# Moving one elementwise operation of the last layer's scans from GpSimd to VectorE

## What is computed

```python
xs  = jnp.stack([xf, xf[..., ::-1], xt, xt[..., ::-1]], axis=1)      # (b, 4, 192, 3136)
dbc = jnp.einsum('bkcl,krc->bkrl', xs, x_proj_w)
dlt, b, c = (dbc[:, :, :R], dbc[:, :, R:R + N], dbc[:, :, R + N:])   # R = 6, N = 16
dlt = jnp.einsum('bkrl,kdr->bkdl', dlt, dt_proj_w) + dt_proj_b[None, :, :, None]
dlt = jax.nn.softplus(dlt)
dA  = dlt[..., None] * A_log[None, :, :, None, :]
phi = jnp.exp(-jnp.cumsum(dA, axis=3))
dbx = dlt[..., None] * jnp.swapaxes(b, 2, 3)[:, :, None] * xs[..., None]
h   = phi * jnp.cumsum(dbx / (phi + 1e-12), axis=3)
y   = jnp.einsum('bkdln,bknl->bkdl', h, c) + Ds[None, :, :, None]
```

## Time and profile before

| | us |
|---|---|
| median of 3 runs | 17136.74 |
| lowest and highest | 17131.63, 17143.35 |
| the profiled execution, its own time | 17136.74 |
| its span, first to last instruction | 17135.0 |
| layer 3's scans, steady stretch of the first pair | 11320 to 13865 |
| layer 3's scans, steady stretch of the second pair | 14292 to 16846 |
| DVE, POOL, PE, ACT busy, share of the span | 89%, 77%, 80%, 70% |

### The profile page before, as it was taken

How to read it: one execution, slowest core, us unless ns; L and a number is a source line. 1 busy time by engine, 2 the same in 40 slices (tenths; PEclk the granted TensorE clock), 3 DMA queues, 4 the chain that set the end, 5 groups by cost and what they waited for, 6 DMA issues and landing times. The chain is left out here.

```text
span 17135.0 us, 184002 instructions
## 1 busy us (share of the span) xinstructions
PE 13644.1 (80%) x38048; PEld 5622.1 (33%) x38048; DVE 15278.8 (89%) x20463; ACT 12036.7 (70%) x24501; POOL 13160.7 (77%) x6369
## 2 busy tenths in 40 slices
PE   7989978888888878888888886977777776777776
PEld 2222233333333333333333333533332332333323
DVE  6666579999999988999999996889999988999998
ACT  3555666667777756666777774578888867888886
POOL 0000069999999978999999994279999977999996
PEclk9999989999999989999999997988888888888898
DMA  1000023333333333333333332222222212222221
GB/s 24 18 14 16 5 87 107 108 107 107 107 107 107 106 93 103 107 108 106 108 107 106 107 107 76 58 73 85 83 81 82 82 48 78 84 83 82 81 82 46
DMA packets 543166, 1404.61 MB, mean 82 GB/s; under 512 B 135566, under 2 KB 191926, under 8 KB 539430
## 3 DMA queue, kind: packets, MB, share of 16 engines
q1 hardware_dynamic: 542034, 1392.84, 28.1%
HBM read 1311.24 MB, written 58.30 MB: 80 GB/s over the span
## 5 line engine op out<-in xcount | busy, mean ns | idle before, releaser
L1067 PE MATMUL PS<-Hc,ident 128*128 128x448 f32 x16128 | 7355.8, 589 | 1945.7 <-POOL Hc L1381 1690.4
L1373 POOL TENSOR_TENSOR Tr<-du,BC 128x1344 f32<-128x1344 f32 x2688 | 8164.8, 3038 | 34.5 <-DVE du L1252 34.4
L1067 PEld LDWEIGHTS PS<-Hc,ident 128*128 128x128 f32 x16128 | 3079.1, 202 | 6125.1 <-POOL Hc L1381 2668.8
L1189 ACT ACTIVATE PS<-dl,A 128x448 f32<-128x448 f32 x5376 | 3402.8, 633 | 2047.8 <-DVE Hr L1290 1247.9
L1381 POOL TENSOR_TENSOR Hc<-Hr,BC 128x448 f32<-128x448 f32 (+1 forms) x2688 | 3895.5, 1449 | 627.2 <-DVE Hr L1290 548.0
L1290 DVE TENSOR_TENSOR_SCAN PS<-PS,st,Tr 128x448 f32<-128x448 f32 x3072 | 3358.5, 1135 | 132.3 <-ACT st L1203 130.1
L1297 DVE TENSOR_TENSOR Hc<-PS,BC 128x448 f32<-128x448 f32 x4480 | 2564.8, 605 | 0.0
L1197 ACT ACTIVATE PS<-cs,lneps,A 128x448 f32<-128x448 f32 x2688 | 1940.1, 722 | 199.3 <-DVE PS L1290 196.1
L1273 DVE SCALAR_TENSOR_TENSOR PS<-PS,Tr 128x448 f32<-128x448 f32 x2688 | 1646.4, 613 | 224.7 <-ACT PS L1197 214.2
L1189 ACT ACTIVATE Ar<-dl,A 128x448 f32<-128x448 f32 x2688 | 1765.0, 657 | 0.0
L1290 DVE TENSOR_TENSOR_SCAN Hr<-PS,st,Tr 128x448 f32<-128x448 f32 x1536 | 1750.4, 1140 | 0.0
(11 more groups left out here) (268 smaller groups left out, 16212.9 us busy)
## 6 DMA issues: line engine op xcount, KB each, us to landing
BC<-bcscratch SPq DMA_DIRECT2D x5376, 224.0 KB, 3.6
zscratch<-zst SPq DMA_DIRECT2D x84, 224.0 KB, 1.9
bcscratch<-rows SPq DMA_DIRECT2D x336, 56.0 KB, 2.9
z<-zscratch SPq DMA_DIRECT2D x28, 672.0 KB, 4.9
xg<-mid SPq DMA_DIRECT2D x12, 1176.0 KB, 7.9
xr<-mid SPq DMA_DIRECT2D x56, 168.0 KB, 2.8
rl<-rows SPq DMA_DIRECT2D x56, 168.0 KB, 3.3
Q<-part SPq DMA_DIRECT2D x72, 98.0 KB, 4.3
```

Source lines behind the costliest of these rows:

```text
L1067: e.matmul(PS[:, YB + c, 0:T], K["ident"][:], Hc[:, g % NHC, c, :], start=False, stop=(nn == 15)).then_inc(y_done, 1)
L1189: e.activation(decay_at(u), dl[:, q % 2, c, :], ACT.Exp, scale=A[:, q // NT, c, nn:nn + 1]).then_inc(a_done, 1)
L1373: e.tensor_tensor(Tr[:, g % NTR], du[:, q % 2], b, ALU.mult).then_inc(t_done, 1)
```

## The change

`one_less` moves from POOL's program (r = 7) to DVE's (s = 22, which is r = 7, c = 1: behind `scan(g, 1)` and before `project(g, 0)`). The instruction, its operands and its semaphores are the same. `prepare` of DVE is called for tile 0 too, for s = 0 to 47.

```diff
@@ dve @@
+            def one_less(q):
+
+                e.wait_ge(expd, 3 * (q + 1))
+                if q:
+                    e.wait_ge(x_full, use(q - 1, "total", 2) + 1)
+                e.tensor_scalar(w1[:], du[:, q % 2], 1.0, 1.0, ALU.add, ALU.subtract).then_inc(minus, 1)
+
...
             def prepare(q, s):
-                if s in (32, 36, 41):
+                if ratio and s == 22:
+                    one_less(q)
+                elif s in (32, 36, 41):
                     (cumsum if ratio else inputs)(q, (32, 36, 41).index(s))
@@ pool @@
-            def one_less(q):
-
-                e.wait_ge(expd, 3 * (q + 1))
-                if q:
-                    e.wait_ge(x_full, use(q - 1, "total", 2) + 1)
-                e.tensor_scalar(w1[:], du[:, q % 2], 1.0, 1.0, ALU.add, ALU.subtract).then_inc(minus, 1)
-
             def prepare(q, r):
-                if ratio and r == 7:
-                    one_less(q)
                 if ratio and 11 <= r < 14:
                     inputs(q, r - 11)
```

## The result

| | us |
|---|---|
| changed kernel, median of 4 runs | 17279.85 |
| the kernel before, median of 4 runs beside it | 17134.19 |
| ratio | 1.0084, 95% interval 1.0069 to 1.0098 |
| so slower by | 144 (118 to 168) |
| spans of the two profiled executions | 17272.7 and 17135.0, difference 137.7 |

The account below looks back on a forecast made before the run. The prediction took DVE to set the pace. 54 held instructions at 2.75 us (+148.5) less 7.7 us in the beginnings gave +141 us on 17136.7, so 17277.5 us, 0.8% slower; range 17200 to 17330.

Parts of the forecast that it names:

- DVE sets the pace, POOL's saving is worth nothing: In the steps, 54 x 4.74 us = 256 us of POOL's time removed, all beside DVE's, so nothing on the path.
- The instruction itself: On DVE, the 128x1344 `tensor_scalar` takes 0.89 us, costing 0.81 us if nothing holds it.
- The rival of the slow rate: On DVE, the instruction runs at the slow rate and isn't held: 1.48 us each, +72 us, 17209; chance 0.08.
- The hold: On DVE, the instruction waits 2.09 us for POOL's `input1`, so the next starts 2.75 us later.
- The delay goes through whole: Behind it in the steps, ACT's block moves too and the 2.96 us pause stays: 54 x 2.75 = +148.5 us.
- The beginnings: At each pair's start, for tile 0, it ends 3.86 us sooner on idle DVE; two times, -7.7 us.
- The rival of the pause: The delay hides in DVE's 2.96 us pause a step later, so steps cost nothing: 17129 us; chance 0.06.

Follow-up runs that it names:

- the thin `one_less`: Against the kernel before: `one_less` stays on POOL but computes 3 of the 1344 columns, the others set to zero once per pair; 17133.95 us, ratio 0.9993.
- the padded `w1`: Changed kernel with two unused columns behind each group of 448 in `w1`; 17207.95 us, ratio 1.0042 against the kernel before.
- s = 21: Changed kernel with `one_less` on DVE one group earlier, behind scan(g, 0); 17202.65 us, ratio 1.0033 against the kernel before.
- s = 23: Changed kernel with `one_less` on DVE one group later, behind scan(g, 2); 17135.67 us, ratio 0.9992 against the kernel before.
- s = 25: Changed kernel with `one_less` on DVE in step r = 8, behind scan(g, 1), before DVE's pause; 17135.51 us, ratio 0.9994 against the kernel before.

## Why the prediction was right

**DVE sets the pace, POOL's saving is worth nothing.** Right as far as can be told: the run with the thin `one_less` gains 12 us (27 to a loss of 3), some 8 of them in the beginnings, and in the changed kernel POOL's idle time grew and the time with it. The share of busy time had POOL ahead; the waits were the view that decided.

**The instruction itself.** 0.89 us from the line between two lengths; measured 0.86 unheld in the beginnings, 0.83 behind a scan. The rival of the slow rate was refused in part because the profile shows the three groups as 1344; this was no argument, since the padded `w1` is printed as 1344 as well.

**The hold.** Expected to end 0.74 us after `input1`, it ends 0.71 after it; 2.75 us of path became 2.73. Both rows it was read from, a 192-element instruction beside a memset and a short one of the convolution stage, carried over to another shape and stage. The Trainium skill's page "SBUF — State Buffer", section "Who interferes with whom", states the exclusion of such a DVE instruction and a GpSimd instruction, first come first served. The positions s = 21, 22 and 23 agree in who waits for whom: DVE 0.6 and 2.0 us, then POOL 0.5. In one point the measurement differs: held, the instruction ends 0.71 us after POOL's, less than its own 0.86, so what is exclusive isn't the whole of the length that the profile shows.

**The delay goes through whole.** Right in the place: the pause is 2.97 us as before, and the block of ACT starts behind the same scan. The steps of the first pair are 75 us longer and those of the second 71, where 74 each were forecast. The small waits are 6 us shorter in the changed kernel's trace, a term that the sum didn't have; its cause is open, as said above.

**The beginnings.** 3.86 us each were expected, 3.66 measured. PE does begin 3.95 us sooner after the table load (1.02 us behind it instead of 4.97), but from there to DVE's first `input2` it is 16.01 us instead of 15.72. It isn't a wait for the logarithms: the 0.41 us in front of PE's L1040 are there in the trace of before as well (at 14281.72), and the logarithms, 1.79 us for all three from 14348.56, are ready by 14350.35. What differs is PE's clock. The stretch from 3.0 to 3.5 us after PE's start, before and then after (the last but two is the granted clock):

```profile
14282.35:14282.85 0.50, 0.50 (x3) 0.27 (x2) 0.00 (x0) 0.00 (x0) 0.00 (x0) 1.00 0.00 0
```

```profile
14351.28:14351.78 0.50, 0.50 (x2) 0.34 (x1) 0.00 (x0) 0.00 (x0) 0.00 (x0) 0.50 1.16 264
```

In both traces PE had been nearly idle, its clock was at the lower of its two levels (0.50, which is 1.2 GHz), and it rose to 1.00 (2.4 GHz) while PE worked: 2.96 us after its start before (at 14282.31), 3.53 us after it in the changed kernel (at 14351.81). The 0.57 us more at half speed are the 0.29 us that went missing. Why it rose later isn't shown. The sum had no term for the clock; that its error was small here is luck.

**The rival of the pause** was refused for s = 22 by the right reason, and the same reason applied at s = 23 would have given the result there; my expectation for that run failed to apply it.

**How near it came.** +141 against +144 is nearer than the measurement can tell, whose interval is 118 to 168. The rows of the trace make it +134, with one term of -6 that the sum lacked.

**Open**: why the small waits for ACT are 6 to 16 us shorter in every kernel that takes `one_less` from POOL, was not tested by itself; and whether s = 23, s = 25 or the thin `one_less` is really faster than before, by 0.2% at most, isn't settled. No version beats the kernel before clearly.

## What to carry to other kernels

A fast-rate `tensor_scalar` from SBUF to SBUF on VectorE waited here for each GpSimd instruction that it fell on (two forms of `tensor_tensor`, and a `memset` in the earlier trace rows), with no semaphore, and the profile counts the wait as busy. Other kinds of GpSimd instructions were not tried. Look for one operation with two very different lengths, and for the place in GpSimd's round where a moved instruction will fall (one group earlier or later made 2.7 us into 1.3 or 0.75). If such an instruction must go to the engine that sets the pace, put it behind the last instruction that the releaser of its next pause waits for; there even 2.7 us cost nothing, in front of a pause of 2.97.

## What was not expected of the hardware

Two unused columns behind each group of 448 turn the rate from 0.86 to 1.52 us for 1344 elements, and take the hold away with it; where GpSimd is busy with instructions of 3 us, the slow rate was the cheaper one (+72 against +144 us).

The hold is mutual, and the one that waits comes next: with VectorE waiting, GpSimd's next instruction, ready to start at once, started 0.05 us before its forerunner's end as elsewhere and was then itself held (3.64 instead of 3.03 us at s = 21).
